# Three reorderings in the opening of a fused state-space, feed-forward, attention and expert kernel

## What is computed

```python
proj = jnp.einsum('bld,pd->blp', hidden_states, in_proj_w)
gate = proj[..., :I]
hbc = proj[..., I:I + CONV_DIM]
dt = proj[..., -H:]
...
for k in range(K):
    conv = conv + pad[:, k:k + L, :] * conv_weight[:, k]
xBC = jax.nn.silu(conv)
...
dt_p = jax.nn.softplus(dt + dt_bias)
A = -jnp.exp(A_log)
dA = jnp.exp(dt_p * A)
dtx = dt_p[..., None] * x
...
yn = (yg * lax.rsqrt(var + EPS)).reshape(B, L, I) * norm_weight
yn = yn * jax.nn.silu(gate)
```

## Time and profile before

| what | us |
|---|---|
| median of 3 timed runs | 1781.15 |
| fastest and slowest of them | 1765.92 and 1786.74 |
| the profiled execution's own time | 1772.24 |
| span of its trace, first to last instruction | 1770.5 |
| PE busy | 1561.6 |
| DVE busy | 1221.4 |
| POOL busy | 942.9 |
| ACT busy | 827.5 |

### The profile page before, as it was taken

One profiled execution on the slowest core, in us unless ns is written; L12 is line 12 of the kernel. 1 busy time (PEld: TensorE's weight loads), 2 busy tenths in 40 slices (PEclk: granted clock), 3 DMA queues, 4 the chain that ended last, 5 costly groups with the idle time before them and its releaser, 6 DMA issues.

```text
span 1770.5 us, 26605 instructions
## 1 busy us (share of the span) xinstructions
PE 1561.6 (88%) x8870; PEld 1227.9 (69%) x8870; DVE 1221.4 (69%) x2024; ACT 827.5 (47%) x1639; POOL 942.9 (53%) x861
## 2 busy tenths in 40 slices
PE   3789999999999999999999759996789999987791
PEld 2567877877878778778787647885557776766581
DVE  5467778777787777787787665556657767768525
ACT  2355554554554545555554323332147666764131
POOL 3257667577576675775766744004544423328444
PEclk9899999999999999999999878998889999998796
DMA  3102111012021110110211012222000000041335
GB/s 115 36 4 81 34 46 61 16 47 62 14 86 27 47 54 17 47 62 12 77 39 43 18 60 72 71 78 77 0 1 13 13 1 1 1 167 72 119 132 166
DMA packets 49497, 92.60 MB, mean 52 GB/s; under 512 B 8016, under 2 KB 32720, under 8 KB 44176
## 3 DMA queue, kind: packets, MB, share of 16 engines
q1 hardware_dynamic: 45744, 79.58, 14.1%
q0 software_dynamic: 3680, 12.06, 2.1%
HBM read 81.14 MB, written 10.49 MB: 52 GB/s over the span
## 4 chain that ended last, share of the span: by engine, by line
PE 61%; DVE 16%; POOL 8%; issue 7%; ACT 4%; DMA 3%; SPq 1%; POOLq 0%; ACTq 0%; DVEq 0%
PE banks L355 31%; PE banks L1726 6%; PE banks L1852 3%; PE banks L1650 3%; PE banks L1644 3%; PE banks L1736 3%; PE banks L1817 2%; POOL wol L360 2%; DMA x<-in_w_gate 2%; DVE tap L1200 2%; PE banks L1842 2%; PE banks L1659 2%; PE banks L1618 2%; DVE acc L623 2%; DVE xbc L1206 1%
## 5 line engine op out<-in xcount | busy, mean ns | idle before, releaser
L1200 DVE SCALAR_TENSOR_TENSOR tap<-banks,parg,tap 128x511 f32<-128x511 f32 (+2 forms) x288 | 215.0, 747 | 41.4 <-ACT tap L927 33.9
L710 POOL TENSOR_TENSOR am<-ah,upto 128x1024 fp32r<-128x1024 f32 x64 | 126.4, 1975 | 214.0 <-PE banks L1618 198.9
L862 POOL TENSOR_SCALAR kz<-kst,head 128x512 fp32r<-128x512 f32 x64 | 99.1, 1568 | 159.9 <-DVE kst L1427 159.9
L355 PE MATMUL banks<-xTh,wch 128*128 128x512 f32 x384 | 163.4, 425 | 7.0 <-DVE em L1304 6.8
L355 PE MATMUL banks<-xTh,wcl 128*128 128x512 f32 x384 | 151.3, 394 | 0.0
L355 PE MATMUL banks<-xTl,wch 128*128 128x512 f32 x384 | 151.1, 394 | 0.0
L1132 ACT ACTIVATE prob<-banks,nmax 128x128 f32<-128x128 f32 (+3 forms) x256 | 121.8, 530 | 54.5 <-DVE nmax L1438 54.4
L935 ACT ACTIVATE th<-tap 128x512 f32<-128x512 f32 x96 | 60.4, 630 | 171.4 <-DVE tap L1200 169.2
L1438 DVE TENSOR_REDUCE nmax<-banks 128x2 f32<-128x256 f32 (+3 forms) x128 | 104.7, 818 | 40.3 <-PE banks L1843 40.2
L710 POOL TENSOR_TENSOR am<-al,upto 128x1024 fp32r<-128x1024 f32 x64 | 121.9, 1904 | 0.0
L927 ACT ACTIVATE tap<-banks,parg 128x512 f32<-128x512 f32 x96 | 74.5, 776 | 91.4 <-PE banks L355 90.4
(11 more groups left out here) (289 smaller groups left out, 4396.7 us busy)
## 6 DMA issues: line engine op xcount, KB each, us to landing
x<-grownT SPq DMA_DIRECT2D x96, 128.0 KB, 4.7
x<-in_w_conv SPq DMA_DIRECT2D x7, 1536.0 KB, 6.5
x<-in_w_gate SPq DMA_DIRECT2D x8, 1024.0 KB, 5.0
x<-in_w_out SPq DMA_DIRECT2D x8, 1024.0 KB, 4.8
eraw<-in_expert_w SPq DMA_DIRECT2D x8, 1024.0 KB, 7.2
gur<-in_ff_gu SPq DMA_DIRECT2D x7, 1024.0 KB, 4.8
x<-in_hidden SPq DMA_DIRECT2D x16, 256.0 KB, 3.8
mates<-yd SPq DMA_DIRECT2D x8, 512.0 KB, 4.4
```

What stands on the lines that cost most here:

```text
L355: m = nc.tensor.matmul(o, a, b, start=first and n == 0, stop=last and n == len(terms) - 1)
L710: m = pool.tensor_tensor(am[:, part, :, :], a[:, i, :].bitcast(F32).unsqueeze(2).to_broadcast([P, HG, P]), upto[:, :].unsqueeze(1).to_broa ...
L862: m = pool.tensor_scalar(kz[:, quad % 2, p2, j, :], kst[:, p2, :].bitcast(F32), head[:, j:j + 1], None, ALU.mult)
L1200: nc.vector.scalar_tensor_tensor(tap[:, q % 2, sh:L], bk(CONV_BANKS[q % 2])[:, 0:L - sh], parg[:, KC * q + k:KC * q + k + 1], tap[:, q % 2 ...
```

## The change

Six moves, and no operation is added or left out.

1. ACT turns from "all weight casts, then the tiles" to "the tiles as they come": tiles 0 to 3, the `wdt` cast, and then one piece of `w_conv` behind each of tiles 3 to 6. `wdt` gets a semaphore of its own, so its cast no longer waits for the small tables.
2. DVE makes `wdtl` within the normalisation (behind the statistics of tile 7) and not behind it.
3. DVE's two small copies that spread `Dskip` (`skip`) go from before the dt chain to behind the first `silu`.
4. ACT casts the gate weights (`gate_high(0)`) behind the two copies of dt and ahead of the first tap, and no longer behind the tanh of tile 1. POOL makes their low parts ahead of the masks of chunk 0, and zeroes the accumulator behind those.
5. PE makes the first gate product in front of the cumulative sums, in bank 1; its tanh and `gate_made` follow the tanh and `silu` of tile 0.
6. Three semaphores are joined with others (`abo_in` and `r_in` to `wide_in`, `table_ready` into `list_ready`) to make room for the new one.

```diff
-            sp.dma_start(wdt[:, :, :], w_dt).then_inc(small_in, 16)
+            sp.dma_start(wdt[:, :, :], w_dt).then_inc(wdt_in, 16)
...
+        def norm_high(q, i):
+            norm_wait(nc.scalar, q, "tr", i + 1)
+            nc.scalar.copy(xTh[:, :, i * P:(i + 1) * P],
+                           bk(i % 2).rearrange("p (k t) -> p k t", k=KT)).then_inc(nsem["hi"], 1)
...
-            norm_wait(pool, 0, "tr", NT)
-            pool.memset(acc[:, :, :], 0.0).then_inc(consts, 1)
...
+            gate_low(0)
             pool.wait_ge(ah_ready, 1)
             decays(0)
-            gate_low(0)
+            norm_wait(pool, 0, "tr", NT)
+            pool.memset(acc[:, :, :], 0.0).then_inc(consts, 1)
...
-            act.wait_ge(wc_in, 16)
-            for k in range(KT):
-                nc.scalar.copy(wch[:, k, :], conv_stage(0)[:, k, :]).then_inc(wc_hi, 1)
-            act.wait_ge(small_in, 16 * 7)
-            nc.scalar.copy(wdth, wdt).then_inc(wdt_hi, 1)
-            norm_scalar(0)
+            for i in range(NT):
+                norm_high(0, i)
+                if i == KT - 1:
+                    act.wait_ge(wdt_in, 16)
+                    nc.scalar.copy(wdth, wdt).then_inc(wdt_hi, 1)
+                    act.wait_ge(wc_in, 16)
+                if i >= KT - 1 and i < 2 * KT - 1:
+                    k = i - KT + 1
+                    nc.scalar.copy(wch[:, k, :], conv_stage(0)[:, k, :]).then_inc(wc_hi, 1)
...
+            gate_high(0)
             act.wait_ge(par_ready, 1)
             first_tap(0, 0)
...
             tanh(0, 0)
+            gate_tanh(1, 1)
...
-                if q == 1:
-                    gate_high(0)
-                if q >= 3:
+                if q >= 4:
                     gate_tanh(q - 2, (1, 7)[(q - 3) % 2])
...
-            norm_vector(0)
-            dve.wait_ge(wdt_hi, 1)
-            low(nc.vector, wdtl, wdt, wdth).then_inc(wdt_lo, 1)
+            def low_dt():
+                dve.wait_ge(wdt_hi, 1)
+                low(nc.vector, wdtl, wdt, wdth).then_inc(wdt_lo, 1)
...
+            norm_vector(0, 0, lambda n: low_dt() if n == NT - 1 else None)
...
             silu(0, 0, 0)
+            gate_made(1, 1, 0, 0)
+            for u in range(2):
+                rows = slice(HP * u, HP * u + HP)
+                nc.vector.tensor_copy(skip[rows, :, :], skip_in[rows, :].rearrange("p (g k u) -> p g k u", k=KT, u=2)[:, :, :, u])
...
             convolved(1, 1, 0)
+            pe.wait_ge(wg_lo, KT)
+            gated(0, 0, 1)
             pe.wait_ge(dve_step, 9)
...
-                if q == 3:
-                    pe.wait_ge(wg_lo, KT)
                 if q == CT - 1:
                     pe.wait_ge(gate_used, 1)
-                if q >= 3:
+                if q >= 4:
                     gated(0, q - 3, (1, 7)[(q - 3) % 2])
```

More of the change, by code:

```diff
@@ L296, in program @@
         at_ps, at_hi, at_lo, ao_ps, ao_ready = (sem(s) for s in ("at_ps", "at_hi", "at_lo", "ao_ps", "ao_ready"))
-        r_in, r_dve, r_act = (sem(s) for s in ("r_in", "r_dve", "r_act"))
-        lg_ps, ch_ready, rank_ps, place_ready, list_ps, list_ready, table_ready = (sem(s) for s in (
-            "lg_ps", "ch_ready", "rank_ps", "place_ready", "list_ps", "list_ready", "table_ready"))
+        r_dve, r_act = (sem(s) for s in ("r_dve", "r_act"))
+        lg_ps, ch_ready, rank_ps, place_ready, list_ps, list_ready = (sem(s) for s in (
+            "lg_ps", "ch_ready", "rank_ps", "place_ready", "list_ps", "list_ready"))
         ew_in = [sem(f"ew_in{n}") for n in range(4)]
@@ L504, in _ @@
             sp.dma_start(out_stage, w_out[0]).then_inc(wo_in, 16)
-            sp.wait_ge(small_in, 16 * 8)
+            sp.wait_ge(small_in, 16 * 7)
             with sp.Fori(0, G - 1) as g:
@@ L682, in norm_tensor @@
                 norm_turn(q, i)
+        def norm_high(q, i):
+            norm_wait(nc.scalar, q, "tr", i + 1)
+            nc.scalar.copy(xTh[:, :, i * P:(i + 1) * P],
+                           bk(i % 2).rearrange("p (k t) -> p k t", k=KT)).then_inc(nsem["hi"], 1)
         def norm_scalar(q):
             for i in range(NT):
-                norm_wait(nc.scalar, q, "tr", i + 1)
-                nc.scalar.copy(xTh[:, :, i * P:(i + 1) * P],
-                               bk(i % 2).rearrange("p (k t) -> p k t", k=KT)).then_inc(nsem["hi"], 1)
+                norm_high(q, i)
         @block.gpsimd
@@ L900, in _ @@
                 pool.wait_ge(xn_out, 16 * NT)
-                pool.wait_ge(list_ready, 1)
+                pool.wait_ge(list_ready, 2)
                 for j in range(GATHERED):
                     gather(j)
-                pool.wait_ge(list_ready, 2)
+                pool.wait_ge(list_ready, 3)
                 for j in range(SLOT_TILES):
@@ L1207, in silu, with gate_made @@
                                                tap[:, q % 2, :], ALU.add, ALU.mult).then_inc(xbc_ready, 1)
-            norm_vector(0)
-            dve.wait_ge(wdt_hi, 1)
-            low(nc.vector, wdtl, wdt, wdth).then_inc(wdt_lo, 1)
-            dve.wait_ge(small_in, 16 * 7)
+            def low_dt():
+                dve.wait_ge(wdt_hi, 1)
+                low(nc.vector, wdtl, wdt, wdth).then_inc(wdt_lo, 1)
+            def gate_made(n, bank, b, j):
+                dve.wait_ge(tg_ready, n)
+                nc.vector.scalar_tensor_tensor(gate_kept(b, j), gt.rearrange("p (a t) -> p a t", a=4), 1.0,
+                                               bk(bank).rearrange("p (a t) -> p a t", a=4), ALU.add, ALU.mult).then_inc(gate_used, 1)
+            norm_vector(0, 0, lambda n: low_dt() if n == NT - 1 else None)
+            dve.wait_ge(small_in, 16 * 6)
             dve.wait_ge(consts, 6)
@@ L1219, in chain @@
                 dve.wait_ge(dve_step, d.n)
-            for u in range(2):
-                rows = slice(HP * u, HP * u + HP)
-                nc.vector.tensor_copy(skip[rows, :, :], skip_in[rows, :].rearrange("p (g k u) -> p g k u", k=KT, u=2)[:, :, :, u])
             chain(nc.vector.tensor_scalar(par[:, :, :], par[:, :, :], 0.5, None, ALU.mult))
@@ L1401, in _ @@
                 add_down(FP - 1, 1)
-                dve.wait_ge(small_in, 16 * 13)
+                dve.wait_ge(small_in, 16 * 12)
                 def values(i):
@@ L1474, in _ @@
                             keys(2 * m + u, i)
-                dve.wait_ge(abo_in, 16)
+                dve.wait_ge(wide_in, 32)
                 for i in range(NT + 1):
@@ L1888, in _ @@
                         if j == 0:
[L1889 removed]
+                            pe.wait_ge(wide_in, 32)
                         norm_wait(pe, 3, "hi", j + 1)
```

24 lines of the change are left out of this document (10 added, 14 removed).

## The result

The changed kernel takes 1758.55 us (median of 4 runs, 1752.98 to 1761.46), the one before 1783.95 (4 runs, 1765.92 to 1787.4). The ratio is 0.9879, 95% interval 0.9839 to 0.9919. On two other occasions the same pair gave 0.991 (0.9877 to 0.9942) and 0.9906 (0.9874 to 0.9939).

A forecast was written before the change was run, and what follows sets the result against it. Bound by a chain of waits in the first 95 us, with PE idle; 9.95 - 0.7 + 9.9 = 19.2, plus 0.9 for the clock, gives 20 us saved; forecast 1757, set between 1752 and 1761, range 1742 to 1773.

The forecast's parts named there:

- Tiles as they come: Normalisation: early ACT copies bring 8.75 us and the dt split inside 1.2, so the dt product starts 9.95 earlier, at 28.6.
- Rival B: Normalisation: DVE's own list order holds the low parts, so early copies bring little; saving 10 us, 1766; chance 0.08.
- Skip copies: Before the dt chain: their 5.43 us lie under the dt product, so taking them away there is worth nothing.
- Collision with `wgl`: Dt chain on DVE: its second step meets POOL's low gate parts and loses 0 to 1.38 us; 0.7 taken.
- Second half without the clock: From third convolution input to group loop: 29.8 us become 19.9, saving 9.9, with the clock over the sums as before.
- Clock over the sums: Cumulative sums on PE: filled idle may hold the full clock, worth 1.9 us since DVE is next; half, 0.9, taken.
- The 1.7 of the upper bound: Group loop's start, 95 to 98 us before: 1.7 us more saved if it keeps its clock, making 23.7.
- Rival A: Taps path stays late: `wgl` ends 2 us later, dt steps and sums wait; costs 3 to 8 us, about 1762; chance 0.13.
- Rival C: Later stages: shifted start brings more half-clock stretches, 1.5 us each; slower than before from 14 more; chance 0.05.
- the same in both kernels: From the group loop's start on nothing differs, so the whole effect is how much earlier that start comes.

The follow-up runs named there:

- second trace of before: The kernel before the change, unchanged, executed once more for its trace; loop opened at 93.05 us, 45.11 from dt to loop; time not read.
- first half alone: Changed kernel with gate casts, low parts, zeroing and first gate product back at their old places; time 0.9942 of before (0.9915 to 0.997).
- repeated trace: The changed kernel executed again, unchanged; loop opened at 73.66 us, 34.47 from dt to loop against 35.22 in its first trace.
- tile 2 first: Changed kernel plus gate casts before dt copies, zeroing before low gate parts, third convolution input before the sums; 0.9859 of before, then 0.9868.
- skip copies back: Changed kernel with the two skip copies back in front of the dt chain; time not read, 35.20 us from dt to loop.

## Why the prediction was right

1757 was forecast and 1758.55 measured. That the two are 1.6 us apart is luck in part: the forecast took a saving of 20 us off a base between 1772 and 1781, the measured medians are 25.4 apart, and on the two other occasions the changed kernel took 1749.77 and 1754.94, 20.4 and 14.8 less than the one before beside it. The traces are the better test: from the first statistics to the opening of the loop 20.6 to 21.1 us are saved against the first trace of before and 18.1 to 18.6 against the second. The mechanism was the forecast one. By its own terms:

- **Tiles as they come, 9.95 us.** From the first statistics to the dt product it was 29.22 (38.53 - 9.31) and is 19.30: 9.92. Against the second trace of before (27.45) it is 8.15: what this half is worth depends on how long behind the first tile `w_conv` lands, which the prediction took from one trace. Rival B, that DVE's own order holds the tiles, is out by the first half alone. What the forecast left out is that the dt product itself may run a shorter or longer time at the lower clock (the 36 matmuls from it on took 9.91 us here and 11.15 in the repeated trace, 10.85 before), a matter of the execution: 29.03 to 30.38 us from statistics to dt over the ten traces with the new order.
- **Skip copies, 0 at their old place.** Putting them back changed nothing under the lower clock; a held clock was not tried. At the new place the prediction had them and the zeroing in front of the taps of tile 2, and so it came where the clock held.
- **Collision with `wgl`, 0.7 taken between 0 and 1.38.** The step took 0.76 more, and its 0.69 again when POOL was moved. Held beside `wgl` was the second dt step (0.69 to 1.45), beside `wcl` and the zeroing the small tables and the skip copies, while the taps from PSUM kept 2.31 for three. With this the rule of the Trainium skill (GPSIMD Engine Reference, Key points), that GpSimd contends with DVE instructions with two SBUF inputs or in a two-port mode, agrees for the inputs; in which mode the copies ran the profile does not show.
- **Second half without the clock, 9.9 us.** From the third convolution input to the loop 29.8 us were to become 19.9. They became 20.1 (73.07 - 52.93).
- **Clock over the sums, 0.9 taken between 0 and 1.9.** Half of the most, so right by the middle and not by a reason. Both cases occurred: a mean of 0.66 in the first trace and 1.00 in the second and third. In the first the way from the sums' start to the fifth input was 11.77 us (59.18 - 47.41), 1.3 less than before. Held, the sums took 3.8 us (3.6 was estimated), and the way from their start to the fifth input 11.06 us (59.78 - 48.72), against the 13.1 of the old pace (10.75 + 2.32): 2.0, where 1.9 was forecast. The second part of the forecast mattered here, that DVE is next and a gain of 3 us at PE is only 2 on the path: the taps of tile 2 were to start 8.9 behind the sums and started 8.69 behind (57.41 - 48.72), straight after the skip copies and the one product, as foreseen. The 1.7 of the upper bound, for the start of the loop, came in the first trace, where the clock held there; in the second it fell again.
- **Rival A, 3 to 8 us for low parts that come 2 later.** Priced too high: with low parts 3.2 later the loop opened 1.2 later, and the sums 2.2. The prediction had four or five dt steps held, and two were; and moving the zeroing, which is how the test made the parts late, gave 1.0 back at the taps of tile 2.
- **Rival C, the clock in the later stages.** It works both ways, with or without the change, and did not make the kernel slower in any of the comparisons. The prediction took the clock for the only source of such steps and 1.5 us for their size. In the traces steps of 2 us stand at full clock, where DVE is held by POOL, and the one of 2.87 is 1.74 of this and the clock only for the rest. So "the same in both kernels" behind the opening of the loop is true of the lists and not of the time: 21.7 us at the opening were 19.3 at the end of the first pair of traces, and 23.7 with the repeated trace of the changed kernel.

The chance for more than 1% was put at 0.63; ratios of 0.988, 0.991 and 0.991 lie on both sides of that bound, so this much was not settled by the measurement. Not tried was a test that fixes the clock; nothing in the kernel sets it.

## What to carry to other kernels

An engine that takes its list in order should not begin with work whose data come late: here eight short copies stood behind a transfer that landed at 18.4 us, and DVE, which waited for the tiles behind them, stood idle for 8.86 us. When two idle places on one engine have different causes, price them apart by points of the trace between them; the savings then add. From dt to the loop two traces of before differed by 0.34 us and three of the changed kernel by 0.75, where the total time of a run scatters by one per cent. Choose such points with care: a distance that begins at the first tile and ends at work that waits for another transfer moved by 2.2 us between two traces of one kernel. And before hiding a product in an idle gap, look at its inputs: having the low parts ready in time was worth 8 us, and the hiding 2 to 3. Before a drift between two traces is put down to the clock, compare the lengths of the single instructions: here much of it was DVE held by POOL.

## What the runs showed of the hardware

- One DVE instruction can be held over two POOL instructions in a row. In "tile 2 first" a copy of 34 numbers per partition took 5.16 us, 30.34 to 35.50 (5.15 in its second trace; the same copy took 0.18 in "skip copies back", with POOL idle): it started beside the last piece of `wcl`, which ended at 32.00, and ended with the zeroing, which ran from 31.94 to 35.46.

```profile
30.34 5.16 DVE L1191 COPY parg<-par 128x34 f32<-128x34 f32 x1
```

- How long it is held can flip between executions. The `silu` of 128x512 took 0.68 to 0.69 us alone, 2.30 when held over one mask, and 4.35 to 4.36 when held over three POOL instructions; it had started 0.16 us behind the start of the mask in the one case and 0.11 in the other (272.03 - 271.87, 274.13 - 274.02).

- The granted clock behind an idle stretch of the same length was not the same from one execution to the next: behind 1.88 us it kept 1.00 once and fell to a mean of 0.66 once. Behind the 2.38 to 2.41 us in front of the sums it fell in two of six traces (the first of the changed kernel, and "skip copies back") and held in four.
